# A five-part transformer kernel on one core: attention probabilities meet the normed context rows before the value weights do

## The reference, cut to what matters

```python
xn = layernorm(x, ln_x_g, ln_x_b)            # context, 257 rows of 384
ln = layernorm(latents, ln_l_g, ln_l_b)      # 32 rows of 512
q = ln @ Wq.T
kv = concatenate([xn @ Wkv.T, ln @ Wlkv.T], axis=1)
k, v = kv[..., :512], kv[..., 512:]          # 8 heads of 64
attn = softmax(where(mask, rmsnorm(q) * SCALE @ rmsnorm(k).T, -max))
out = (attn @ v) @ Wo.T + bo
```

## Time and profile before

| what | us |
|---|---|
| median of 3 runs (1898.42 to 1904.56) | 1903.61 |
| the profiled execution, its own time | 1904.64 |
| its span, first to last instruction | 1902.9 |
| TensorE busy | 1631.2 (86% of the span) |
| VectorE busy | 1289.5 (68%) |
| ScalarE busy | 954.4 (50%) |
| GpSimd busy | 629.6 (33%) |

### The profile page before, as it was taken

The page is one execution under the profiler, slowest core; times in us unless marked ns, Lnnn a source line. Parts: engine busy times, 40 slices in busy tenths (PEclk is TensorE's granted clock), DMA queues, the critical chain, the costliest instruction groups (busy, mean ns, idle before and its releaser), DMA issues. The chain is left out here.

```text
span 1902.9 us, 43704 instructions
## 1 busy us (share of the span) xinstructions
PE 1631.2 (86%) x15542; PEld 1114.3 (59%) x15542; DVE 1289.5 (68%) x2906; ACT 954.4 (50%) x2170; POOL 629.6 (33%) x762
## 2 busy tenths in 40 slices
PE   6959999999985788669999999679996299989996
PEld 3525555555553566547777777435543277777775
DVE  7858888888875677548888888577666754454441
ACT  4635565655653344236666666433332355555551
POOL 4535555555541111021111111135453123323332
PEclk9989999999996899779999999789998599999998
DMA  5111110111121000021111110421000575565512
GB/s 196 42 59 32 31 42 31 33 39 31 42 81 60 1 2 2 1 76 33 33 33 33 33 33 25 177 97 29 12 13 12 202 200 154 154 187 150 144 30 69
DMA packets 50064, 126.40 MB, mean 66 GB/s; under 512 B 6913, under 2 KB 19553, under 8 KB 49889
## 3 DMA queue, kind: packets, MB, share of 16 engines
q1 hardware_dynamic: 44914, 112.64, 18.3%
q0 software_dynamic: 5008, 11.80, 3.2%
HBM read 110.83 MB, written 15.68 MB: 66 GB/s over the span
## 5 line engine op out<-in xcount | busy, mean ns | idle before, releaser
L107 PE MATMUL e_pGU<-XT,WB 128*128 128x128 f16 x1344 | 232.2, 222 | 20.4 <-issue 10.9
L108 PE MATMUL e_pGU<-XT,WB 128*128 128x128 f16 x1344 | 232.1, 222 | 0.0
L109 PE MATMUL e_pGU<-XT,WB 128*128 128x128 f16 x1344 | 231.9, 222 | 0.0
L2540 DVE SCALAR_TENSOR_TENSOR WB<-w5in,WB 128x1024 f16<-128x1024 f32 x96 | 115.5, 1223 | 85.9 <-ACT WB L2682 85.8
L107 PEld LDWEIGHTS e_pGU<-XT,WB 128*128 128x128 f16 x1344 | 133.6, 99 | 24.0 <-issue 22.5
L108 PEld LDWEIGHTS e_pGU<-XT,WB 128*128 128x128 f16 x1344 | 133.6, 99 | 3.3 <-issue 1.8
L109 PEld LDWEIGHTS e_pGU<-XT,WB 128*128 128x128 f16 x1344 | 133.6, 99 | 0.0
L107 PE MATMUL dpK<-dLT,W 128*128 128x256 f16 x384 | 106.1, 276 | 18.4 <-POOL dLT L1644 18.4
L2523 POOL TENSOR_TENSOR XT<-e_mf,XT 128x256 f16<-128x256 f32 x84 | 56.3, 671 | 174.4 <-ACT XT L2696 174.4
L710 POOL TENSOR_TENSOR crn<-css,mhalf 128x8 f32<-128x8 f32 x64 | 106.7, 1667 | 5.3
L1655 POOL TENSOR_TENSOR XT<-dzo,XT 128x128 f32 (+1 forms) x32 | 13.7, 428 | 283.9 <-ACT XT L1800 283.9
(11 more groups left out here) (536 smaller groups left out, 5655.6 us busy)
## 6 DMA issues: line engine op xcount, KB each, us to landing
w5in<-in_WE SPq DMA_DIRECT2D x96, 512.0 KB, 4.6
cx<-in_ctx SPq DMA_DIRECT2D x32, 384.0 KB, 3.2
dx<-in_ctxT SPq DMA_DIRECT2D x32, 384.0 KB, 3.1
w5in<-in_W SPq DMA_DIRECT2D x14, 512.0 KB, 8.8
wpiece<-in_W SPq DMA_DIRECT2D x12, 512.0 KB, 9.2
w3in<-in_W SPq DMA_DIRECT2D x11, 512.0 KB, 9.4
v<-vlat SPq DMA_DIRECT2D x32, 96.0 KB
X<-in_x SPq DMA_DIRECT2D x8, 256.0 KB, 8.3
```

Of the source, the lines that this page charges most:

```text
L107: pe.matmul(out, lh, rh, start=first, stop=False, skip_group_check=shared)
L108: pe.matmul(out, lh, rl, start=False, stop=False, skip_group_check=shared)
L109: return pe.matmul(out, ll, rh, start=False, stop=last, skip_group_check=shared)
L2540: dve.scalar_tensor_tensor(WB[w][:, 1, a], ring[n][:, :], WS, WB[w][:, 0, a], ALU.mult, ALU.subtract)\
```

## The change

- **First cross-attention.** The value projection of the context goes. The normed rows themselves (`yb`, split by `rows_high` on ScalarE and `rows_low` on GpSimd) are multiplied with the probabilities (`mix`: per group of heads 18 matmuls of 128 columns), and the mix is split into `U` (`mix_high`, `mix_low`). For four batches together, the value weights with the norm's gain folded in (`Wg`, made once by `fold_scale`, `fold_sum`, `fold_high`, `fold_low`) are multiplied with the mixes of two heads in `outputs(p)`, once per batch step: 18 matmuls of 128 columns, each to a strip of 64 partitions, 4 with the bias row (`base`, `minus`) and 8 with the latents' value rows. Its result is evacuated by one `out_high` and one `out_low` of 128 by 128.
- Key buffers, sums, squares and banks exist twice, one for each half. The copy to the high part of the context moves from VectorE (`high`) to ScalarE (`context_high`). The scaling of the tail probabilities (`thrice`) is two instructions in place of one.
- The hardware loop goes: every engine has straight code over the steps -2 to 38, in each of which it handles stages of several batches. `outputs` of a four-batch group follow its mixes over the next four steps.
- SyncE: the tail buffers are 8 (`RING`), and `tail(b)` waits for `outputs`; the pieces of `w3in` are one tile whose space `U`, `yb` and the fold use in the meantime, so that they come in four parts, behind the last readers.
- **Polynomial attention.** GpSimd does `pattern_low(3)` before `rotate(3)`; `turn_norm("a")` comes before `attend`, `turn_mat(2)` and its splits go to the slot's end.

```diff
-    def project(q, u, i, dst, at, free, made):
-        pe.wait_ge(sig[free], q + STARTS[free])
+    def mix(b, g):
+        if g:
+            pe.wait_ge(sig["c0_ulo0"], b + 1)
+        else:
+            pe.wait_ge(sig["c0_ptlo"], b + 1)
+            pe.wait_ge(sig["c0_ylo"], b + 1)
+        for k in range(XK):
+            for i in range(2):
+                m = product(pe, pP[:, k * P:(k + 1) * P], hl(yb[:, b % 4], i, slice(k * P, (k + 1) * P)), hl(PT, g, i), i == 0, i == 1)
...
+    def outputs(p):
+        n, c4 = p // CK, p % CK
...
+        if p:
+            pe.wait_ge(sig["c0_olo"], p)
...
+        for k in range(XK):
+            for a, w in ((0, 0), (1, 0), (0, 1)):
+                for j in range(2):
+                    h = 2 * c4 + j
+                    pe.matmul(strip(j), Wg[:, w, k, h * HD0:(h + 1) * HD0], U[n % 2][:, a, g, k, h % HG, :], ...)
...
+    for s in STEPS:                      # TensorE
+        if on(s - 2): scores(s - 2)
+        if on(s - 1): turn_key(s - 1, 0); keys(s - 1, 1, 0 to 2)
+        if on(s + 1): turn_context(s + 1)
+        if on(s):     keys(s, 0, 0)
+        if on(s - 2): turn_probs(s - 2)
+        if on(s):     keys(s, 0, 1); keys(s, 0, 2)
+        if on(s - 2): mix(s - 2, 0)
+        if on(s - 1): turn_key(s - 1, 1)
+        if on(s - 6): outputs(s - 6)
+        if on(s - 2): mix(s - 2, 1)
...
+    for s in STEPS:                      # VectorE
+        out_low(s - 7); softmax_max(s - 2); stats(s + 2); softmax_scale(s - 2)
+        squares(s - 1, 1); key_low(s - 1, 0); probs_low(s - 2); tail_low(s - 2)
+        key_scale(s - 1, 1); squares(s, 0); mix_low(s - 2, 0); key_low(s - 1, 1)
+        norm(s + 2); mix_low(s - 2, 1); key_scale(s, 0)
...
+    for s in STEPS:                      # ScalarE
+        out_high(s - 7); gather(s - 1); key_high(s - 1, 0); exps(s - 2)
+        square(s - 1, 1); affine(s + 1); probs_high(s - 2); tail_high(s - 2)
+        square(s, 0); context_high(s + 1); mix_high(s - 2, 0); key_high(s - 1, 1)
+        rows_high(s + 1); mix_high(s - 2, 1)
...
+    for s in STEPS:                      # GpSimd
+        rms(s - 1, 0); gather_keys(s - 1); context_low(s); rows_low(s)
+        power(s + 2); rms(s - 1, 1)
```

(The four step lists are shown without their `if on(...)` where it says nothing more.) In `poly`, on TensorE:

```diff
                     values(b)
-                    turn_mat(2, b)
+                if t is not None:
+                    turn_norm("a", t, ya)
                 if q is not None:
                     wait_after("p_xo", min(s + 1, NT))
...
                     attend(q)
-                if t is not None:
-                    turn_norm("a", t, ya)
                 if r is not None:
...
+                if b is not None:
+                    turn_mat(2, b)
```

More of the change, by code:

```diff
@@ L648, in cross0 @@
         maskrow = st["maskrow"]
[L650 to L660, removed]
+        hl = lambda t, *ix: (t[(slice(None), 0, *ix)], t[(slice(None), 1, *ix)])
@@ L670, in tail @@
[L670 to L692, removed]
+                sp.dma_start(cx[b % 2][:, :, :], d["ctx"][b, 0:FULL, :].rearrange("(i p) n -> p i n", p=P))\
+                  .then_inc(sig[f"cx_in{b % 2}"], 16)
@@ new lines, in tail @@
+            def tail(b):
+                if b >= RING:
+                    sp.wait_ge(sig["c0_q"], CK * ((b - RING) // QUAD) + CK)
+                sp.dma_start(v3[0:3 * S, b % RING, :], st["vlat"][b * 3 * S:(b + 1) * 3 * S, :]).then_inc(sig[f"v3_in{b % RING}"], 16)
+                sp.dma_start(v3[3 * S:TAIL, b % RING, :], st["vrem"][b * 3:b * 3 + 3, :]).then_inc(sig[f"v3_in{b % RING}"], 16)
+            context(0)
+            context(1)
+            for b in range(RING):
+                tail(b)
@@ new lines, in _, with weights @@
+            for b in range(2, B + 3):
+                if b < B:
+                    context(b)
+                if b - 3 >= RING:
+                    tail(b - 3)
+            widths = st["W3cols"]
+            at = [sum(widths[:n]) for n in range(len(widths))]
+            def weights(n):
+                first = WAT["o0"] + at[n]
+                sp.dma_start(st["W3in"][n][:, :], d["W"][:, first:first + widths[n]]).then_inc(st["kept"][f"w3_in{n}"], 16)
+            for n in range(9, 12):
+                weights(n)
@@ L851, in after, with tail_low @@
-            def after():
-                softmax_scale(B - 2)
-                value_low(2 * B - 1, 1, 1)
-                probs_low(B - 2)
-                key_low(2 * B - 1, 1, 1)
-                out_low(B - 2)
-                softmax_max(B - 1)
-                softmax_scale(B - 1)
-                probs_low(B - 1)
-                out_low(B - 1)
-            dve.wait_ge(sig["c0_const"], 3)
-            walk(dve, body, before, after)
+            def tail_low(b):
+                dve.wait_ge(sig["c0_ptthi"], b + 1)
+                rest = PTt[:, b % RING, :, :]
+                dve.scalar_tensor_tensor(rest, rest, third[0:TAIL, :], turned, ALU.mult, ALU.add).then_inc(sig["c0_pttlo"], 1)
@@ new lines, in biases @@
+            def biases():
+                pe.wait_ge(sig["c0_lblo"], 1)
+                for k in range(XK):
+                    m = product(pe, pS[0:TAIL, 0, :], hl(lb, k), hl(W, k, slice(D, 2 * D)), k == 0, k == XK - 1)
+                m.then_inc(sig["c0_bias"], 1)
+            for s in STEPS:
+                if on(s - 2):
+                    scores(s - 2)
+                if on(s - 1):
+                    turn_key(s - 1, 0)
+                    for k in range(XK):
+                        keys(s - 1, 1, k)
+                if on(s + 1):
+                    turn_context(s + 1)
+                if on(s):
+                    keys(s, 0, 0)
+                if on(s - 2):
+                    turn_probs(s - 2)
+                if on(s):
+                    keys(s, 0, 1)
+                    keys(s, 0, 2)
+                if on(s - 2):
+                    mix(s - 2, 0)
+                if on(s - 1):
+                    turn_key(s - 1, 1)
+                if on(s - 6):
+                    outputs(s - 6)
+                if on(s - 2):
+                    mix(s - 2, 1)
+                if s == 0:
+                    biases()
```

606 lines of the change are left out of this document (337 added, 269 removed).

## The result

The changed kernel takes **1886.0 us** (median of 4 runs, 1882.9 to 1887.4) against 1902.9 for the kernel before beside it: 0.991 of it, interval 0.990 to 0.993. It is faster by 17 us where 42 were forecast. The profiled execution took 1886.4 us, with a span of 1884.7.

A forecast was written before the change was run, and what follows sets the result against it. TensorE's own work was taken as the bound, plus waits on a single key bank. Steps of 12.5 us with fill and end start `middle` at 544.5 instead of 587.25, so 1904.6 - 42.7 = 1862 us; range 1832 to 1892.

The forecast's parts named there:

- Fill: Start of the cross-attention: first sum of squares as before within 0.5 us, first full step at about 137.5.
- -3 with what the fold adds: Cross-attention steps: four of the 30 at 12.5 us have no outputs, taking 3 us off, the fold's cost included.
- behind the small negation: VectorE in a cross-attention step: after maximum and negation, two statistics of 1.00 us each, done at 5.05.
- the walk: One cross-attention step followed from the scores' start: about 12.5 us, 11.2 of TensorE work and 1.3 of new waits.
- Neither binds by its sum: ScalarE at 9.2 and GpSimd at 9.0 us busy per cross-attention batch would not set the step.
- scores to second mix 11: End of the cross-attention: the last batch, alone, takes 11 us from its scores to its second mix.
- four outputs ... 2.1 us each, with the clock down: End of the cross-attention: four last outputs, each waiting for the split of the one before, 2.1 us each.
- TensorE's own work: Cross-attention batch on TensorE: 12.8 - 4.8 + 2.0 for mixes + 1.2 for outputs = 11.2 us.
- the turns are alike, so the chains stay. I take 0: Polynomial steps: swapping one turn of four transposes for another in both gaps changes nothing; bounds -4 to +3 us.
- More waits: Rival: strips of 64 don't overlap or GpSimd's list delays the second half's scaling; 13.4 a step, 1889 us; chance 0.25.
- Slower: Rival: new idle places drop the clock to 1.2 GHz; one step in four so gives about 1935 us; chance 0.04.
- Weights for `middle`: Start of `middle`: three weight pieces asked for only after the last outputs cost 0, at most 3 us.

The follow-up runs named there:

- run 13: Changed kernel with each of GpSimd's two remainders (context and rows) issued in two halves, VectorE keeping its negation: 1890.4 us, 0.994 of the kernel before.
- run 9: Changed kernel with the softmax's negated maximum made on ScalarE instead of VectorE: 1872.2 us, 0.984 of the kernel before.
- Runs 6: Changed kernel with the four bias matmuls of the outputs ordered base, base, minus, minus: 1884.8 us, 0.991 of the kernel before.
- run 10: Changed kernel with the negation on ScalarE and the bias matmuls ordered base, base, minus, minus: 1863.3 us, 0.980 of the kernel before.
- run 7: Changed kernel with the last three outputs written to banks of keys, without waiting for the previous output's split: 1887.4 us, 0.993 of the kernel before.
- run 4: Changed kernel with the polynomial stage ordered as before, so the new cross-attention alone: 1898.5 us, 0.9985 of the kernel before.
- run 5: Changed kernel with VectorE's negation as a multiplication by a tile of constants instead of an immediate: 1887.5 us, 0.993 of the kernel before.
- run 11: Changed kernel, negation on ScalarE, normed rows ahead of the softmax scaling, row remainder last in GpSimd's list: 1871.8 us, 0.984 of the kernel before.

## Why the prediction was wrong, and where it was right

**Direction and range held; the size did not.** 42.7 us were forecast for the stage and 7.1 came, a gap of 35.6. The score starts of the changed kernel divide it: the first at 139.35, the fifth at 197.05, the thirtieth at 526.33 and the last at 550.56.

- *Fill*: 139.35 where I said 137.5: 1.9 us.
- *First four steps*: 57.7 us where 4 x 12.5 - 3 = 47 were taken: 10.7. The failed step is "-3 with what the fold adds": four steps without outputs of 1.2 us would save 4.8, so it leaves the fold of weights and constants 1.8 us that were not worked out. Neither part held. In the step of 16.5 us (153.77 to 170.26) VectorE's remainder of the folded weights takes 2.13 us over GpSimd's 2.09, and TensorE waits 3.40 for the probabilities. In run 13, with GpSimd's remainders in halves, such a remainder takes 1.40 and 0.70, the negation isn't held in these steps (0.17 to 0.28), and the four take 51.8 us. The third and the fourth, with a remainder of 0.70 in each and nothing held, take 12.26, some 0.3 less than run 9's usual step with outputs, where the term has 0.75 a step. The two rows of the changed kernel, then one of run 13:

```profile
156.72 2.13 DVE L838 TENSOR_TENSOR cWg<-w3in,cWg 128x512 f16<-128x512 f32 x1
```

```profile
156.21 2.09 POOL L727 TENSOR_TENSOR w3in<-cy,w3in 128x768 f16<-128x768 f32 x1
```

```profile
168.08 0.70 DVE L841 TENSOR_TENSOR cWg<-w3in,cWg 128x512 f16<-128x512 f32 x1
```

- *The 25 steps to 526.33*: 13.17 each, 16.8 us more than at 12.5. The failed step is "behind the small negation", for which the walk leaves 0.25 us (2.0 + 0.8 + 2 x 1.00 is 4.8, and I wrote 5.05) and the trace shows 0.60, and with it "Neither binds by its sum": GpSimd has 9.0 us busy in 13.24, as forecast, but its long instruction stops VectorE at one point of every step. Runs 6, 9 and 10 show that this tie set the step: TensorE's saving of 0.3 us counts only with the negation off VectorE, and with that the 25 steps take 12.59 on average, which is 14.6 of the 16.8 us. The usual 12.53 is the value of my walk partly by luck: in run 9's step from 309.21 TensorE waits about 0.8 us by the starts where the walk has 1.3, and its outputs and mixes take more than I had. The tie closes a loop, and its pieces can be followed through the rows of one step without a gap: from the remainder's end (306.41) over the negation, statistics, softmax scaling and sum of squares on VectorE (to 310.25), GpSimd's two steps for the second half, the scaling and the next sum of squares (to 313.64), again GpSimd's two steps, its copies and both remainders, to 319.66. That is 13.25 us, and in run 13 it grows by just what the halves add. VectorE's and GpSimd's timelines, where the loop passes from one to the other:

```profile
312.36 0.69 DVE L779 SCALAR_TENSOR_TENSOR ckh<-cpK,crn 128x512 f32<-128x512 f32 x1
312.97 0.67 DVE L773 TENSOR_REDUCE css<-csq 128x8 f32<-128x512 f32 x1
```

```profile
313.73 0.25 POOL L732 TENSOR_SCALAR css<-css 128x8 f32<-128x8 f32 x1 [1.40 <-DVE css L773]
```

- *The last two steps*: 24.2 us, where 12.5 + 11.6 and the microsecond for the context load make 25.1: 0.9 less.
- *The end*: 29.6 us from the last scores to `middle` where I had 20.5 + 1.8 = 22.3. Two terms failed. The larger is "scores to second mix 11": the first of the four outputs starts at 565.75, 15.2 us behind the scores, 4.2 more. Behind an idle time of 3.46 us (before 556.03) the clock is at half, the 1.2 GHz level, so the 18 matmuls of the first mix take 2.0 us instead of 1.0 (558.99 to 561.02) and the outputs behind them 2.0 instead of 1.2 (to 563.00). The split of the second mix, 1.8 us to 565.75, was in no term. The other is "four outputs ... 2.1 us each, with the clock down", 9.5 in all: they take 11.4, and stand 3.04 apart. At half of full clock their 18 matmuls take 0.93, each of the four bias matmuls stands 0.24 from the next, and the split of the output before adds 0.75 of idle time; in run 7, without that wait, they stand 2.15 apart. The remaining 1.1 lie between the last output and `middle`. TensorE's timeline, and its windows (columns as the earlier trace rows):

```profile
558.99 0.29 PE L106 MATMUL cpP<-cPT,w3in 128*128 128x128 f16 x1 [1.41 <-DVE cPT L809]
...
561.02 1.17 PE L1106 MATMUL cpO<-w3in,cWg 128*64 128x128 f16 x18
...
565.75 1.17 PE L1106 MATMUL cpO<-w3in,cWg 128*64 128x128 f16 x18 [1.57 <-DVE XT L828]
...
568.79 1.17 PE L1106 MATMUL cpO<-w3in,cWg 128*64 128x128 f16 x18 [0.75 <-issue]
```

```profile
556.00:560.00 4.00, 2.55 (x16) 2.21 (x17) 1.08 (x2) 0.87 (x2) 0.00 (x0) 0.50 0.00 0
...
570.00:575.00 5.00, 3.51 (x46) 2.48 (x47) 0.58 (x2) 0.55 (x2) 0.00 (x0) 0.50 0.51 202
```

1.9 + 10.7 + 16.8 - 0.9 + 7.3 is 35.8, the gap to within rounding.

**TensorE's own work** was right but for one term. The outputs take 1.42 us (300.45 to 301.87), not 1.2. The 18 matmuls to two strips take 0.53, so the strips share the time. The four bias matmuls stand 0.15 to 0.17 apart, where a matmul of 128 columns in a stream takes 0.055. The Trainium skill (TensorEngine Tiling (Array Packing), Key Properties) says that a change of tiling mode drains the array; the rows here show about 0.1 us for each, and grouped by shape (run 10) the four take 0.32 us together instead of 0.66. The mixes keep the pace of the earlier trace rows, 0.055, and not the 81 ns that the prediction quotes from the Trainium skill (TensorE: Matmul & The Clock Gate, Back-to-back issue gap).

**The `poly` steps** fell at "the turns are alike, so the chains stay. I take 0". I read the idle time of 1.17 by the releaser named, a split that `attend` doesn't need, which ended at the same hundredth as the one it does need, and never looked at GpSimd's list, which the diff changed in one place. The bound of -4 was wrong as well: it was worth 12. That hides part of the miss on the cross-attention, which by run 4 leaves the kernel at 1898.5 alone, outside the range.

**The rivals.** *More waits*, 13.4 a step, is near what the step became (13.2), for another reason than the two it named: strips of 64 overlap, and GpSimd's list delays the second half only through the hold on VectorE. *Slower*, by a fall of the clock, did not come in the steady part: it is 1.00 with idle times of 0.99 us. (The 1935 of that rival doesn't follow from its own figures: one in four of 30 steps, 10.8 us longer each, adds 81 to 1862.) Weights for `middle` didn't delay its start, as forecast: ScalarE's first eight pieces are 7.68 us there as before.

## What to carry to other kernels

Sum of busy time does not say that two engines are independent. Where VectorE and GpSimd both run, compare the minimum, median and maximum of each short VectorE instruction in the tile view; a spread with ends that fall on the end of a GpSimd instruction points to a wait that no semaphore shows, and moving the held instruction to ScalarE may free more than it costs. Where an idle time has a releaser, look in the code whether the waiting instruction reads that very buffer (the profile leaves buffer numbers out), and what else ended at that moment; and cost every line of a reordering on the engine it is on, not only on the one that waits. An edit that brings nothing is worth trying again once a tie elsewhere is cut: the bias order brought 0 and then 9 us.

## What the runs showed of the hardware

A VectorE instruction of 128x2 that takes 0.17 us alone took up to 1.35 us while a GpSimd subtraction was under way, and ended with it within 0.04 us; with that subtraction cut in two it took at most 0.89. Held in this way were some instructions that read SBUF alone: scalings by an immediate or by scalars (`cnm`, 0.60; `cy`, 2.27 for two in place of 0.86), the one with two SBUF tiles of run 5 (0.60), and the subtraction of the folded weights (2.13 in place of 0.70). GpSimd's own subtraction took 2.09 there in place of 1.64. Not held were those that read PSUM beside at most one SBUF tile (the maximum, 0.76 at 305.03; a mix remainder, 0.56 at 303.61, both over a remainder on GpSimd), and two kinds that read one SBUF tile and no PSUM: the statistics (0.55 at 311.94 in run 9) and the sum of squares (0.68 at 315.19 in run 11, over a remainder from 314.52 to 316.17). Nor does every GpSimd instruction hold: before, the negation took its 0.17 us (300.25) inside a power of 1.67 (299.74), and the two scalings of the rows take 0.86 at 301.95 over such a power. The trace of before already had one case of the hold, at 117.92, ahead of the loop. VectorE's and GpSimd's timelines:

```profile
117.92 2.18 DVE L137 TENSOR_SCALAR cy<-cx,mv,rs 128x384 f32<-128x384 f32 x2
```

```profile
118.08 1.80 POOL L703 TENSOR_TENSOR cLT<-cz,cLT 128x768 f16<-128x768 f32 x1 [0.65 <-DVE cLT L752]
```

The Trainium skill (GPSIMD Engine Reference, Specifications) says that GpSimd shares its SBUF interfaces with VectorE, with contention for VectorE instructions in a 2-port performance mode or with two SBUF inputs. The trace agrees with the list of what was held and what was not, as far as its second half goes (run 5, the folded weights, and the instructions that read PSUM); in which mode the scalings run no row shows. What costs 14 us here is that a short instruction waits for the end of a long one.
